# Expert-pair loops of a mixture-of-experts kernel: written out on TensorE, VectorE and ScalarE instead of counted loops

## The reference

```python
x = x + _L0_ffn_ref(_L0_cond_ref(x, cond, w0), w_gate, w_up, w_down)
x = x + _L1_ffn_ref(_L1_cond_ref(x, cond, Wx, Wh, b), router_w, w1, b1, w2, b2)
# _L1_cond_ref: a recurrence over 128 time steps
next_h = jnp.tanh(xw_t + prev_h @ Wh)
# _L1_ffn_ref: 8 experts, each with a hidden width of 512, mixed by the two best of a router
h1 = jax.nn.gelu(jnp.einsum('bth,efh->btef', x, w1) + b1, approximate=False)
expert_outputs = jnp.einsum('btef,ehf->bteh', h1, w2) + b2
```

## Time and profile before

| | |
|---|---|
| runs | 301.69, 301.76, 303.23 us, median 301.76 us |
| the profiled execution | span 301.2 us from its first to its last instruction |
| TensorE busy | 264.4 us (88%), weight loads 205.5 us |
| VectorE busy | 258.8 us (86%) |
| ScalarE busy | 215.6 us (72%) |
| GpSimd busy | 76.2 us (25%) |
| matmuls in the trace | 2716 |

### The profile page before, as it was taken

The page is one execution under the profiler, slowest core; times in us unless marked ns, Lnnn a source line. Parts: engine busy times, 40 slices in busy tenths (PEclk is TensorE's granted clock), DMA queues, the critical chain, the costliest instruction groups (busy, mean ns, idle before and its releaser), DMA issues.

```text
span 301.2 us, 8834 instructions
## 1 busy us (share of the span) xinstructions
PE 264.4 (88%) x2716; PEld 205.5 (68%) x2716; DVE 258.8 (86%) x635; ACT 215.6 (72%) x455; POOL 76.2 (25%) x148
## 2 busy tenths in 40 slices
PE   4969940049989999999999999999999999999994
PEld 4824440016956777778888788888777887888874
DVE  4888999989898897779988799887799988889885
ACT  6367899998842677767777676667566766689892
POOL 3367997000025413011302112212110311101000
PEclk9989976557999999999999999999999999999999
DMA  6990443101500000000000000000001000001000
GB/s 186 314 310 4 84 94 76 28 0 35 90 17 2 0 3 1 0 2 2 19 0 0 2 3 26 2 0 0 1 2 30 8 0 0 2 1 37 0 2 27
DMA packets 24031, 10.63 MB, mean 35 GB/s; under 512 B 13355, under 2 KB 22982, under 8 KB 24006
## 3 DMA queue, kind: packets, MB, share of 16 engines
q1 hardware_dynamic: 23470, 10.05, 13.6%
q10 hardware_dynamic: 536, 0.26, 0.3%
HBM read 6.11 MB, written 1.05 MB: 24 GB/s over the span
## 4 chain that ended last, share of the span: by engine, by line
PE 79%; DVE 16%; issue 1%; ACT 1%; DMA 1%; SPq 0%; DVEq 0%
PE bank L893 78%; DVE peak L706 3%; DVE big L728 3%; DVE peak L633 2%; DVE big L711 1%; DVE big L744 1%; PE bank L937 1%; DMA y_sb<-in_cond 1%; PE bank L1017 0%; DVE big L746 0%; DVE wyT L779 0%; DVE pkm L626 0%; DVE big L738 0%; DVE x_sb L759 0%; DVE q L700 0%
## 5 line engine op out<-in xcount | busy, mean ns | idle before, releaser
L893 PE MATMUL bank<-big,wt 128*128 128x384 f16 (+2 forms) x480 | 124.8, 336 | 0.6 <-DVE big L872 0.5
L893 PE MATMUL bank<-wt,big 128*128 (+1 forms) x1536 | 111.5, 219 | 0.1
L872 DVE TENSOR_TENSOR big<-big 128x384 f16<-128x384 f32 (+2 forms) x160 | 93.2, 585 | 20.5 <-ACT big L594 16.1
L893 PEld LDWEIGHTS bank<-wt,big 128*128 128x128 f16 x1536 | 97.9, 97 | 16.2 <-issue 0.2
L592 ACT ACTIVATE big<-bank,miscT 128x384 f32<-128x384 f32 (+2 forms) x160 | 96.2, 602 | 15.3 <-PE bank L893 8.2
L893 PEld LDWEIGHTS bank<-q,wxh 128*128 128x128 f32 x254 | 44.4, 189 | 17.4 <-issue 3.4
L893 PEld LDWEIGHTS bank<-big,wt 128*128 (+1 forms) x480 | 50.0, 117 | 4.8 <-issue 1.1
L580 ACT ACTIVATE q<-bank (+1 forms) x112 | 20.6, 184 | 38.7 <-PE bank L893 37.9
L404 POOL CAST big<-q 128x64 f16<-128x64 f32 x32 | 13.2, 413 | 129.0 <-ACT q L580 126.5
L868 DVE CAST big<-big 128x512 f16<-128x512 f32 (+2 forms) x104 | 38.6, 372 | 4.8 <-ACT big L592 3.9
L827 DVE SCALAR_TENSOR_TENSOR wyT<-bank,gates,wyT 128x128 f32<-128x128 f32 x128 | 39.8, 343 | 1.0 <-issue 0.6
(11 more groups left out here) (165 smaller groups left out, 320.0 us busy)
## 6 DMA issues: line engine op xcount, KB each, us to landing
wnat<-in_w SPq DMA_DIRECT2D x8, 512.0 KB, 7.7
x_sb<-in_x SPq DMA_DIRECT2D x4, 256.0 KB, 4.3
out_block<-wyT SPq DMA_DIRECT2D x15, 64.0 KB
wn<-in_w_gate ACTq DMA_DIRECT2D x1, 192.0 KB, 4.9
wn<-in_w_up SPq DMA_DIRECT2D x1, 192.0 KB, 5.6
wn<-in_w_down SPq DMA_DIRECT2D x1, 192.0 KB, 5.7
b_in<-in_b SPq DMA_DIRECT2D x12, 4.0 KB
wt<-wyT SPq DMA_TRANSPOSE x8, 3.0
```

The lines of the kernel that those rows point to most:

```text
L872: V.tensor_tensor(g_lo[:, par, f, 0:w], g32[:, f, 0:w], g_hi[:, par, f, 0:w], ALU.subtract).then_inc(g_lo_done, 1)
L893: return nc.tensor.matmul(o, l, r, start=start, stop=stop, skip_group_check=True)
```

## The change

The loops go. `chunks` calls `pair` for each chunk and each `e2` as a plain number, so all 20 pairs are straight-line code on all three engines; addresses and counts become constants. Tests that told a loop's body from straight-line code by the type of `e2` become tests of its value. What each pair computes, in which order on each engine, and the counts that are waited for stay the same.

```diff
-        def chunks(eng, pair):
+        def chunks(pair):
             for c in range(CH):
-                pair(c, 0, c > 0)
-                with eng.Fori(1, E // 2 - (c == CH - 1)) as e2:
-                    pair(c, e2, True)
-            pair(CH - 1, E // 2 - 1, True)
-
-        def is_first(e2):
-            return isinstance(e2, int) and e2 == 0
+                for e2 in range(E // 2):
+                    pair(c, e2, c > 0 or e2 > 0)
+
+        def is_last(c, e2):
+            return c == CH - 1 and e2 == E // 2 - 1
...
             def pair(c, e2, prev):
-                first = is_first(e2)
+                first = e2 == 0
...
-                    if isinstance(e2, int) and not first and s == 3:
+                    if is_last(c, e2) and s == 3:
                         take_gates(c)
...
-            chunks(act, pair)
+            chunks(pair)
...
             def earlier_slot(c, e2, prev, s):
-                first = is_first(e2)
+                first = e2 == 0
                 f, par = s % NF, s // NF
                 slot = c * SLOTS + e2 * 2 * NF + s
                 if prev or s >= NF:
-                    e = e2 * 2 + par - 1 if not first else (E - 1 if par == 0 else 0)
+                    e = (e2 * 2 + par - 1) % E
...
-            chunks(pe, pair)
+            chunks(pair)
```

More of the change, by code:

```diff
@@ L233, in program @@
         o_lo = gate2.bitcast(F16)[:, NJ * TOK:2 * NJ * TOK]
-        def chunks(eng, pair):
+        def chunks(pair):
             for c in range(CH):
-                pair(c, 0, c > 0)
-                with eng.Fori(1, E // 2 - (c == CH - 1)) as e2:
-                    pair(c, e2, True)
-            pair(CH - 1, E // 2 - 1, True)
-        def is_first(e2):
-            return isinstance(e2, int) and e2 == 0
+                for e2 in range(E // 2):
+                    pair(c, e2, c > 0 or e2 > 0)
+        def is_last(c, e2):
+            return c == CH - 1 and e2 == E // 2 - 1
         def added_before(c, e2, par):
-            if is_first(e2):
+            if e2 == 0:
                 return LATE + E * START[c] // P - (2 - par) * TILES[c - 1]
@@ L855, in pair @@
                         add_b2(c - 1)
-                    if isinstance(e2, int) and not first and s == 6:
+                    if is_last(c, e2) and s == 6:
                         add_b2(c, 2)
@@ L879, in pair @@
                         mark_experts(c)
-            chunks(dve, pair)
+            chunks(pair)
             dve.wait_ge(b2_added, CH)
@@ L1140, in pair @@
                         mix_b2(c - 1)
-                    if isinstance(e2, int) and not first and s == 2:
+                    if is_last(c, e2) and s == 2:
                         transpose_gates(c)
-                    if isinstance(e2, int) and not first and s == 4:
+                    if is_last(c, e2) and s == 4:
                         mix_b2(c)
```

## The result

The changed kernel takes 298.07 us (median of four, 297.84 to 298.48), the kernel before beside it 302.24 us (301.69 to 303.23): a ratio of 0.985, 95% interval 0.983 to 0.987. Repeated later, with five runs, it was 297.71 us against 302.79, ratio 0.983 (0.981 to 0.985). One run of all that follow, with VectorE and ScalarE alone written out, took 326.75 us at a granted clock of 0.817, where the others show 0.94 to 0.96, and is left out of that kernel's median. It runs 7122 instructions instead of 8834.

What follows compares the result with a forecast made beforehand. TensorE was taken to bound the kernel, its sequencer's register work making it late in narrow chunk 0. Chunk 0's 4.5 us plus 0.5 us from chunk 1, 5.0 us off the 301.76 us median, gave 296.8 us, range 295.7 to 299.0.

Steps and rivals of the forecast that it cites:

- the rival in which VectorE holds chunk 0 back harder: In chunk 0 VectorE's pair takes 6.6 us instead of 6.1, losing 1.2 us more: 298.0 us, chance 0.17.
- Register work in chunk 0: TensorE's register operations and loop turns in chunk 0 are removed, so slots fall to 0.80 and 0.66 us: 5.10 us saved.
- the later losses: Waits behind VectorE in chunk 0, about 0.4 us once and 0.2 us for slower casts, leaving 4.5 us.
- the slot at the loop's entrance: TensorE's slot entering chunk 0's loop took 0.87 us, 0.07 above the pace, to be saved.
- Removed, at no gain of their own: Register work and branches on ScalarE and VectorE go without separate gain, as both have time left in each pair.
- the straight-line pace: TensorE's pace in chunk 0's first pair: 0.80 us a slot with a recurrence step, 0.66 without, 6.12 us a pair.
- VectorE next: In chunk 0's second pair TensorE waits about 0.4 us, once, for VectorE's late subtraction.
- The pace that VectorE was to set with TensorE: In chunk 0 VectorE needs 6.1 us a pair against TensorE's 6.12; slower casts cost 0 to 0.45 us, taken as 0.2.
- Leaving chunk 0: At TensorE's exit from chunk 0's loop the next matmul starts 0.17 us late, to be saved.
- Loop turns in chunk 1: Loop turns in chunk 1's three looped pairs cost 0.17, 0.20 and an estimated 0.1 us: 0.47 us saved.
- Longer code: Nine more bodies on each engine, costed at 0; at most 9.3 us if nine more packets are each waited out.
- The branch: Rival that only loop turns' compare-and-branches cost: 300.7 us, or 300.3 us by the skill's 108 ns; chance 0.04.

Runs made afterwards that it cites:

- TensorE alone: Against the kernel before, only TensorE's pairs were written out, while VectorE and ScalarE kept their loops: 298.65 us, ratio 0.988.
- the sequencer work put back: Changed kernel plus eight already-met wait instructions a slot on TensorE in chunk 0's last three pairs: 301.89 us; with four a slot 298.94 us.

## Why the prediction was right

The forecast of 296.8 us missed the 298.07 us by 1.3, and the range held it. By the number alone the rival in which VectorE holds chunk 0 back harder, 298.0 us, came true. The trace speaks against it: it wanted pairs of 6.6 us, and the third takes 6.13. The case that came is the forecast's own. Step by step, in the stretch:

- *Register work in chunk 0.* Forecast 5.10 us with the later losses apart. Measured: the slot at the loop's entrance 0.08 with its pair, third pair 7.86 - 6.14 = 1.72 (forecast 1.74), second pair 1.43, fourth pair with the way out 0.97 (forecast 1.04 + 0.17). The second pair's slot behind VectorE took 1.44 us instead of 0.80; without that the pair gave the 2.08 us forecast. That TensorE was late and not the tanh is shown by the sequencer work put back, and by TensorE alone giving 3.64 us.
- *The part of ScalarE.* "Removed, at no gain of their own" is the step that failed. For VectorE it holds. For ScalarE it was right only as long as TensorE was late: its register work, between tanh and gelu above all, costs 1.02 us as soon as TensorE is fast. The sum was not harmed, since the straight-line pace already contained a straight-line ScalarE. Idle time on ScalarE did not show this; what counted was how late one short instruction of it, the tanh, came.
- *VectorE next.* The place was right, the size was not: a pause of 0.64 us, where 0.4 was forecast. TensorE starts 0.06 us after the subtraction ends, and the forecast put that at nothing (its low half "near 109.15" is 109.13 us by its own terms). VectorE's cast of slot 6 took 0.36 us and the two subtractions 0.82 together, with 0.29 and 0.43 each in the earlier trace rows; GpSimd was splitting states at that moment, which it did later before. In the repeated profile GpSimd was at it too, and the cast and the first subtraction took their usual time:

```profile
107.83 0.37 POOL L402 CAST big<-q 128x64 f16<-128x64 f32 x1 [2.63 <-ACT q L578]
108.28 0.45 POOL L404 TENSOR_TENSOR big<-q,big 128x64 f16<-128x64 f32 x1
```

```profile
107.82 0.30 DVE L866 CAST big<-big 128x256 f16<-128x256 f32 x1
108.15 0.87 DVE L870 TENSOR_TENSOR big<-big 128x256 f16<-128x256 f32 x2
```

The second subtraction took 0.53 us there. By the distances between starts TensorE waited 0.46 us for the first and 0.10 for the second. So most of the pause is VectorE's usual lateness; the longer instructions beside GpSimd were seen and not tried by themselves. The 0.14 us at the fourth pair's start, which the forecast lacked, are a wait for ScalarE's tanh, late behind two gelus, of which the first started 0.34 us after the tanh before it instead of 0.12; why is open.

```profile
120.91 0.30 PEld L891 LDWEIGHTS bank<-q,wxh 128*128 128x128 f32 x2 [0.15 <-ACT q L578]
```

The pace that VectorE was to set with TensorE, 0.2 us, didn't come apart from that: the third pair runs at TensorE's 6.13 us.
- *Leaving chunk 0.* 0.17 us forecast, 0.08 measured. The first matmul of the input part still starts 0.43 us after the six products begin, 0.09 later than the forecast's 0.34, in the changed kernel too:

```profile
125.79 0.50 PE L891 MATMUL bank<-wt,big 128*128 128x128 f16 x6
126.22 0.39 PE L891 MATMUL bank<-ones,bh_rows 33*128 33x512 f16 x1
```

- *Loop turns in chunk 1.* 0.47 us forecast and measured (0.17 + 0.19 + 0.11). They are not TensorE's alone, as the forecast had it: with TensorE still in loops, writing out the two others took 0.38 us of them away. Chunks 2 to 4: unchanged to 0.01 us a pair.
- *Longer code.* Cost 0, as taken. Seven more packets came on that queue, nine were assumed, and no pause of a matmul over 0.15 us is listed from 128 to 294 us. "About three times the code" was too much: eleven pairs of code became twenty. The Trainium skill's "mostly hidden" (Runtime: NRT & Kernel Launch, Instruction fetch mechanics) holds here for twenty pairs in a row.
- *The branch.* The Trainium skill's 108 ns for a compare-and-branch (Advanced Engine Details and Errata, Control Flow Timing), by which the turns were worth 1.5 us by estimate, misses the point here. The branch took 208 ns in the median, but chunk 0 alone gave 3.89 us, and putting sequencer work back without a single branch took the whole gain away.

The sum in the stretch was then 4.66 us where 5.0 was forecast. The larger part of the miss lies outside it: "I take the saving off the median" started from 301.76 us, and with a fourth run that kernel's median was 302.24. And the medians differ by 4.17 us only, 0.5 less than the stretch; in the repetition, 302.79 to 297.71, they differ by 5.08. The 0.56 us taken for what lies around the span was wrong too, at no cost to the forecast. Where a run's span is listed, its time lies 1.7 to 1.9 us above it (297.71 for 295.9; 302.90 for 301.1 before), but for three runs with chunk 0 alone written out. By that the profiled execution of before, at 301.2, was one of about 303 us, and median and span came from different executions.

## What to carry to other kernels

Judge an engine's sequencer by its instructions in the slot, each times its spacing, against the time of the slot: here eight at 0.106 us cost nothing in a 1.45 us slot and undid the whole gain in one of 0.80 us. So write out the narrow part of a loop nest first; the wider chunks gave only 0.47 us of 4.66. And when a late sequencer goes, look for the short instruction that was hidden behind it: here a tanh on ScalarE, a subtraction on VectorE.

## What was not expected

VectorE's loop costs nothing (156.90 us with and without it when the others are written out, 157.92 and 157.93 when ScalarE keeps its loop), though VectorE is the next engine in line. The two sides' loops mask each other in chunk 1, where writing out either was enough or nearly so. And the first block, identical in all kernels, brings chunk 0 to its first slot anywhere between 100.07 and 101.87 us, which is most of the scatter between runs of one kernel as far as the profiles show it; what differs there was not studied.
